# Layer 0 of a graph network: where a chunk's maxima are turned and reduced on TensorE and VectorE

## The reference

```python
h = x @ Wx.T + bx
q, k, v = h @ Wq.T + bq, h @ Wk.T + bk, h @ Wv.T + bv
e = concat([edge_attr, cos(abs(node_vec[src] - edge_weight)[:, None] * time_w + time_b)]) @ We.T
alpha = sum(q[dst] * (k[src] + e), -1) / sqrt(128)
amax = segment_max(alpha, dst)                 # a maximum over the edges of each node
alpha = exp(alpha - amax[dst])
alpha = alpha / (segment_sum(alpha, dst)[dst] + 1e-16)
m = segment_sum((v[src] + e) * alpha[:, None], dst)
x1 = layernorm(x + tanh(h + tanh(h @ A.T + m + b_ac)))
```

## Time and profile before

| | us |
|---|---|
| median of the runs | 4160.7 |
| span of the profiled execution | 4156.7 |
| TensorE busy, share of the span | 3100.8 (75%) |
| VectorE busy | 2472.7 (59%) |
| ScalarE busy | 1733.9 (42%) |
| GpSimd busy | 3014.0 (73%) |
| first and last gather of layer 0 start at | 53.27 and 2011.18 |
| first gather of layer 1 starts at | 2175.20 |

### The profile page before, as it was taken

The page is one execution under the profiler, slowest core; times in us unless marked ns, Lnnn a source line. Parts: engine busy times, 40 slices in busy tenths (PEclk is TensorE's granted clock), DMA queues, the critical chain, the costliest instruction groups (busy, mean ns, idle before and its releaser), DMA issues. The chain is left out here.

```text
span 4156.7 us, 73778 instructions
## 1 busy us (share of the span) xinstructions
PE 3100.8 (75%) x18778; PEld 2820.4 (68%) x18779; DVE 2472.7 (59%) x5456; ACT 1733.9 (42%) x2900; POOL 3014.0 (73%) x3193
## 2 busy tenths in 40 slices
PE   6888887888888888888666666666667677766675
PEld 4777777777777777777546666666666666666665
DVE  4877777777777777777574444444444444454544
ACT  3767776777777777777461111111111111111111
POOL 5777777777777777777347777777777777777775
PEclk8999999999999999999896666666666666767677
DMA  6333333333333333333233333333333333333332
GB/s 187 81 81 83 81 83 81 83 81 82 82 81 82 81 82 82 81 82 82 75 102 101 89 92 89 92 89 91 91 89 93 91 96 93 94 95 94 94 95 61
DMA packets 419860, 370.13 MB, mean 89 GB/s; under 512 B 269651, under 2 KB 347883, under 8 KB 419724
## 3 DMA queue, kind: packets, MB, share of 16 engines
q0 software_dynamic: 100032, 217.87, 20.5%
q1 hardware_dynamic: 308544, 143.31, 13.5%
q10 hardware_dynamic: 11214, 8.17, 0.7%
HBM read 347.56 MB, written 21.44 MB: 89 GB/s over the span
## 5 line engine op out<-in xcount | busy, mean ns | idle before, releaser
L721 POOL DMA_INDIRECT he<-h_table,src_i x1563 | 1477.5, 945 | 515.7 <-issue 505.3
L1642 POOL DMA_INDIRECT msg<-p_table,src x1563 | 1474.8, 944 | 484.1 <-issue 484.1
L1659 PE MATMUL p_edge<-r_win,hotT 80*128 80x128 f32 x3136 | 656.7, 395 | 589.2 <-DVE msg L1780 575.2
L1659 PEld LDWEIGHTS p_edge<-r_win,hotT 80*128 80x128 f32 x3136 | 606.6, 297 | 630.5 <-issue 536.8
L1715 ACT ACTIVATE msg<-msg 128x1024 f32<-128x1024 f32 x196 | 207.2, 1057 | 1649.0 <-DVE msg L1780 1649.0
L1780 DVE TENSOR_TENSOR msg<-msg,p_edge 128x512 f32<-128x512 f32 x392 | 251.9, 684 | 979.1 <-DMA msg<-p_table,src 979.1
L1670 PE MATMUL p_sumT<-msg,hot 128*80 128x129 f32 x3136 | 601.0, 372 | 34.4 <-ACT sumT L1723 34.4
L1670 PEld LDWEIGHTS p_sumT<-msg,hot 128*80 128x80 f32 x3136 | 580.0, 224 | 51.3 <-issue 51.2
L760 PE MATMUL p_score<-qk_two,heT 128*128 128x160 f32 x1568 | 394.9, 335 | 166.2 <-ACT heT L870 164.4
L762 PE MATMUL p_score<-qk_win,heT 128*128 128x80 f32 x3136 | 462.7, 272 | 0.0
L762 PEld LDWEIGHTS p_score<-qk_win,heT 128*128 128x128 f32 x3136 | 451.9, 199 | 0.0
(11 more groups left out here) (205 smaller groups left out, 4114.8 us busy)
## 6 DMA issues: line engine op xcount, KB each, us to landing
dst_row<-in_dst_dram SPq DMA_DIRECT2D x196, 320.0 KB
feat<-in_edge_attr_dram SPq DMA_DIRECT2D x196, 128.0 KB
he<-h_table,src_i POOLq DMA_INDIRECT x1563
msg<-p_table,src POOLq DMA_INDIRECT x1563
qk_win<-qk_table SPq DMA_DIRECT2D x196, 40.0 KB
qk_two<-qk_table SPq DMA_DIRECT2D x392, 20.0 KB
r_win<-r_table SPq DMA_DIRECT2D x196, 40.0 KB
qk_table<-qk SPq DMA_DIRECT2D x13, 512.0 KB
```

Source lines behind the costliest of these rows:

```text
L721: e.indirect_dma_start(out=he[u][:, j, 2 * FE:2 * FE + ROW], out_offset=None, in_=h_table[:, :], in_offset=bass.IndirectOffsetOnAxis(ap=sr ...
L1642: e.indirect_dma_start(out=msg[u][:, j, 0:D], out_offset=None, in_=p_table[:, :], in_offset=bass.IndirectOffsetOnAxis(ap=src_i[u][:, j:j + ...
L1659: mm = e.matmul(p_edge[h][:, j % 4, :], hotT_of(c)[:, j, :], r_win[u][:, :], start=True, stop=True)
```

## The change

On TensorE, `turn_top(c)` is moved behind `scores(c+1)`, and it waits in addition for `level_done` of chunk c-1, since it writes the PSUM tensor which the level of that chunk reads. On VectorE, the maximum over a partition's edges is taken out of `masks` into a function of its own, `tops_of_edges`; `tops_of_nodes(c)` and `diagonals(c)` are moved from the top of the step to behind `masks(c+1)`, and `tops_of_edges(c+1)` is last.

```diff
@@ TensorE: turn_top(c)
                             e.wait_ge(top_j_done, val(e, n + 1))
                             again(e, top_n_done, val(e, n))
+
+                            again(e, level_done, val(e, n))
                             e.transpose(p_topT, top_j[:, :], ident[:, :]).then_inc(topT_full, 1)
@@ TensorE: step(c)
                             if not is_first(c):
                                 spread_top(shift(c, -1))
-                            turn_top(c)
                             if not is_last(c):
                                 scores(shift(c, 1))
+                            turn_top(c)
                             if behind(c, 3):
                                 turn_back(shift(c, -3))
@@ VectorE: masks(c)
                                                        in1=p_score[h][:, :, :], op0=ALU.mult, op1=ALU.add).then_inc(masked[h], 1)
+
+                        def tops_of_edges(c):
+
+                            n1 = val(e, count(c) + 1)
                             for h in range(2):
                                 e.wait_ge(masked[h], n1)
                             e.tensor_reduce(top_j[:, :], score_of(c)[:, :, :].rearrange("p j w -> p w j"), AX_X, ALU.max).then_inc(top_j_done, 1)
@@ VectorE: step(c)
                             pick_start(c)
-                            tops_of_nodes(c)
                             if not is_last(c):
                                 places(shift(c, 1))
-                            diagonals(c)
                             if behind(c, 4):
                                 add(shift(c, -4), starts[4])
...
                             if not is_last(c):
                                 others(shift(c, 1))
                                 masks(shift(c, 1))
+                            tops_of_nodes(c)
+                            diagonals(c)
+                            if not is_last(c):
+                                tops_of_edges(shift(c, 1))
@@ VectorE: ahead of the loop
                         masks((0, 0))
+                        tops_of_edges((0, 0))
```

## The result

The changed kernel takes 4174.89 us (median of 7 runs, 4171.85 to 4180.68) against 4162.89 (7 runs, 4159.37 to 4166.52): 1.0031 times before, interval 1.0022 to 1.0041. It is 12 us slower, where no difference was forecast, and above the forecast's range. The profiled execution is the slowest of the seven, 4180.68 us with a span of 4178.2; that of before has a span of 4156.7. A run's time is 1.7 to 3.0 us above its span in the seven runs of the changed kernel, so that of before is among the fastest by this estimate.

The account below looks back on a forecast made before the run. GpSimd's gathers, 10.0 us a chunk, were taken to bound layer 0. Profiled span 4156.7 - 0.2 (start) + 1.7 (tail) = 4158.2, plus 4.0 from span to median: 4162.2 us, range 4156 to 4168.

Parts of the forecast that it names:

- What bounds the kernel: Layer 0: GpSimd's gathers set the pace at 10.0 us a chunk, and the other engines follow.
- The wait removed: TensorE: `turn_top` no longer waits for VectorE's reduce, 0.13 us a chunk; gains nothing while TensorE follows the gathers.
- The steps moved: VectorE's reordered step: 0 us a step, bounds -0.6 and +0.3; the level about 0.45 us earlier.
- The wait added: TensorE: `turn_top` waits for the previous chunk's level; sums and turn come some 0.7 us later, bounds 0.3 and 1.3.
- Who notices?: Later sums in layer 0: GpSimd has about 7 us of cover, VectorE 2.5, so the 0.7 us cost nothing.
- The pace of 1.250 us: GpSimd in layer 0: gathers start an even 1.250 us apart, and do so again after the change.
- The start: Wait for chunk 0's sums before chunk 7's gather: -0.2 us, bounds -1.0 and +0.5.
- The tail: From layer 0's last gather to its end: +1.7 us, bounds 0.3 and 2.5, from a later `turn_back` in the last step.
- the last `add` against the last gather: Sign at the end of layer 0: the last `add` comes 1 to 2 us later relative to the last gather.
- D: Rival for the whole time: nothing of the change reaches the end, 4160.5 us; chance 0.12.
- E: Rival: GpSimd's slots run out again soon after the start, one more stall of 5.5 us, 4167.7 us; chance 0.045.
- B: Rival: the added wait lowers TensorE's clock in every step, +157 us, 4318 us; chance 0.025.

Follow-up runs that it names:

- edges last: Changed kernel with SyncE issuing a chunk's window rows and source indices ahead of its edges' loads; 4169.54 us, 1.0002 times the kernel before.
- late turn: Changed kernel with `turn_top` issued on TensorE behind the sums of two chunks before instead of ahead of them; 4173.32 us, 1.0014 times the kernel before.
- second small kernel: Separate kernel without the layer: stages of 40 gathers beside one VectorE instruction about every 1.1 us, then chunks with edge loads placed differently; no ratio to the kernel before.

## Why the prediction was wrong

- **What bounds the kernel** held: on the first chip GpSimd's gathers set layer 0's pace, before and after.
- **The wait removed** costs and gains nothing: right. **The steps moved** likewise, as far as VectorE's own length goes: its wait for rows fell only from 235.1 to 210.5 us in 150 chunks. But the level, forecast 0.45 us earlier behind the rows' arrival, is 0.11 earlier at the median.
- **The wait added** was described rightly up to its end: the transpose waits for the level, sums come later (0.95 us at the median, forecast 0.7 with bounds of 0.3 and 1.3), GpSimd doesn't wait for them. It read both places in one step, 3.65 and 4.21 us behind the rows' arrival, where the medians are 3.37 and 3.91. The step that failed is **"Who notices?"**. It asked which engine would *stop* for 0.7 us and went through GpSimd and VectorE. It left out SyncE, whose `load_edges` waits for the same sums and has no 7 us of cover: it issues at once. And it costed a delay that ends in spare time at nothing, as though only lateness could cost. On this chip what counts is where things fall. Its term, 0, measured +10.9 us of long gathers out of +15.0 between chunk 7 and the last gather; at layer 1's rate of 2.4 ns a gather 3.6 of the rest are no effect of the change.
- **The pace of 1.250 us** was taken as a constant of GpSimd. It was a mean that held 21 collisions, and the rows from which the argument took it do not show durations one by one; a count of them would have.
- **The start**: the sums' wait shrank by 1.45 us, forecast 0.2, beyond the bound of 1.0. The sign was right, the size was too small. But the wait is 5.36 us in the trace of edges last and 2.43 in that of the late turn, so it differs more between kernels and executions than the forecast's term, and one trace does not confirm the reasons.
- **The tail**: +1.7 forecast, +1.9 measured between the two layers' gathers in this trace. The sign that the prediction named, the last `add` against the last gather, moved by 1.0 (36.3 to 37.2 us). In the two variants the distance between the gathers grew by 4.4 and 4.6, in one trace each, so the agreement is not worth much.
- **Behind layer 1** nothing was forecast, and all three traces of changed kernels show the last two sums at 3.70 us each under a granted clock of 0.50, and end 3.5 us later than the one of before, where it is 0.78. The 3.5 us go with TensorE's lower clock, in code that the change does not touch. Four executions don't tell whether this is chance; it stays open.
- **Rivals.** D (nothing) and E (slots run out) lie too low, and E's stall did not come. B named a slower clock; between 1000 and 1600 us it fell from 0.96 to 0.94, and TensorE's busy time did not grow (490.77 to 487.78 us). None was the one that happened: that was no wait and no new bound, but a longer bounding instruction. On the chips with stops E's kind of mechanism is real, with 31 stops of GpSimd for sums and 239.6 us against 26 and 127.5 (the one ahead of chunk 7, 49.1 and 51.3, is in both). The cover is used up in the step where the loop turns, for which the prediction had counted 7 us.

What is shown and what is argued: that VectorE with two SBUF inputs makes gathers longer, and by how much for a given start, is shown by itself. That the loads' place beside the last gather makes rows late and puts VectorE there is supported by one intervention in the kernel (1.0002, with the sums as late as in the changed kernel), in which the window's loads moved as well, and by the chunks' division in four traces. That the late sums move the loads is supported by the late turn, which gives back half (1.0014). The rest stays unexplained: no run has VectorE's new order without the added wait, or the wait without the order. The changed kernel itself did not run on the last chip, so its 1.0031 and the variants' ratios come from two chips, each against its own runs of before (4162.89 and 4166.38 us). Why four chips stop the engines about once a chunk stays open, too.

## What to carry to other kernels

When an engine that issues gathers sets the pace, its instructions' duration is part of the forecast: list the single durations, see which of VectorE's instructions run at the starts of the long ones, and ask of a change whether it moves VectorE against the gathers' cycle, even by 0.2 or 0.3 us. For a delayed signal, list *everything* that waits for it, the queues of loads too, and ask not only who stops but what will now run side by side. Take the places from medians over many steps, not from one. And a wait put ahead of work that a bounding engine needs is safe only where the worst step of the loop leaves cover, which may be used up on another chip.

## What the runs showed of the hardware

- An indirect gather of 128 rows takes 0.944 us. If it starts at least 0.05 us behind the start of a VectorE instruction with two SBUF inputs (80 to 256 columns, or tensor_scalar from fp32 SBUF) and over 0.13 us ahead of its end, it ends 0.81 to 0.83 us behind that end: in the four traces of chips where the gathers set the pace 257 of 257 such gathers from 140 us on, of up to 1.19 us, and 33 of 33 in the second small kernel. Starts at 0.15 to 0.16 behind L945 (0.43 us long) were long in 42 of 42, 1.087 us on average; at 0.06 to 0.10 behind a fade (0.33 us long) in 30 of 30, 1.070.
- Where both start within 0.02 us, the gather keeps its length and the fade takes 0.371 us in place of 0.328 (10 cases).
- Back to back such instructions can keep one gather waiting until the last of them is done, 23.47 us here; one with a PSUM input costs it nothing (0.944).
- Rows gathered on GpSimd land 1.6 to 1.7 us behind the end of the last gather, and 1.98 on average (1.82 to 2.26, 70 chunks of the changed kernel) where SyncE issues three loads (the largest 128 KB) from 0.0 to 0.4 us behind that gather's start.
- One and the same kernel takes 4163 to 4166 us on two chips and 5172 to 5233 on four others, where GpSimd stops about once a chunk, for 2.8 us on average in layer 0.
